# A selective scan on one core: the side chain of a unit moved to the first half of the unit ahead, and delta*u made by GpSimd

## The reference, cut to what matters

```python
xi, z = jnp.split(x @ in_w.T, 2, axis=-1)
xc = lax.conv_general_dilated(..., conv_w, (1,), [(D_CONV - 1, 0)], feature_group_count=D_INNER)
u = jnp.swapaxes(jax.nn.silu(xc + conv_b[None, :, None]), 1, 2)
x_dbl = u @ xproj_w.T                      # dt (8 columns), B (16), C (16)
delta = jax.nn.softplus(dt @ dt_w.T + dt_b)
A = -jnp.exp(Alog)
dA = jnp.exp(jnp.einsum('bld,dn->bldn', delta, A))
dBu = jnp.einsum('bld,bln,bld->bldn', delta, Bm, u)
h = a * h + b;  y_t = einsum('bdn,bn->bd', h, c)      # the scan, over t
y = y + u * Dp
return y * jax.nn.silu(z) @ out_w.T
# the block: out = concatenate([fw(x) + x, flip(bw(flip(x)) + flip(x))]) @ proj_w.T + proj_b, then a layer norm
```

## Time and profile before

| | us |
|---|---|
| median of 3 runs | 4233.08 |
| the profiled execution | 4230.57 |
| its span, first to last instruction | 4228.6 |
| VectorE busy in the span | 2663.5 (63%) |
| TensorE busy | 3369.4 (80%) |
| ScalarE busy | 1794.7 (42%) |
| GpSimd busy | 1184.5 (28%) |

### The profile page before, as it was taken

One profiled execution on the slowest core, in us unless ns is written; L12 is line 12 of the kernel. 1 busy time (PEld: TensorE's weight loads), 2 busy tenths in 40 slices (PEclk: granted clock), 3 DMA queues, 4 the chain that ended last, 5 costly groups with the idle time before them and its releaser, 6 DMA issues. The chain is left out here.

```text
span 4228.6 us, 48168 instructions
## 1 busy us (share of the span) xinstructions
PE 3369.4 (80%) x12573; PEld 1552.5 (37%) x12573; DVE 2663.5 (63%) x4056; ACT 1794.7 (42%) x2759; POOL 1184.5 (28%) x974
## 2 busy tenths in 40 slices
PE   5599986999985699877896777867777669558998
PEld 2122225444443354444443332323223243533443
DVE  6788854333345577554334999999999853454444
ACT  2166642444435255433333655556565413212222
POOL 3211110000002222100002888878888700100000
PEclk7699996999988799878897889888898969769999
DMA  4512110000006533100002333333333210000000
GB/s 136 124 59 65 54 41 1 0 0 0 0 28 172 128 93 87 47 0 0 0 0 82 127 124 121 134 116 130 120 131 122 98 38 0 2 0 0 0 0 20
DMA packets 131080, 253.84 MB, mean 60 GB/s; under 512 B 24773, under 2 KB 100954, under 8 KB 113434
## 3 DMA queue, kind: packets, MB, share of 16 engines
q1 hardware_dynamic: 126842, 250.55, 18.3%
q0 software_dynamic: 4096, 1.59, 0.2%
HBM read 191.98 MB, written 56.89 MB: 59 GB/s over the span
## 5 line engine op out<-in xcount | busy, mean ns | idle before, releaser
L1626 PE MATMUL a_y<-a_g,ident 128*128 128x512 f32 x1024 | 563.4, 687 | 275.9 <-POOL a_g L1906 256.9
L1906 POOL TENSOR_TENSOR a_g<-a_g,a_spread 128x1024 f32<-128x1024 f32 x256 | 662.2, 2600 | 176.1 <-DVE a_g L1839 174.3
L941 DVE TENSOR_REDUCE a_top<-a_sc 128x1 f32<-128x512 f32 (+3 forms) x1024 | 545.1, 585 | 168.9 <-PE a_sc L818 96.2
L1839 DVE TENSOR_TENSOR_SCAN a_g<-a_decay,a_drive 128x512 f32<-128x512 f32 x512 | 592.3, 1201 | 36.3 <-ACT a_drive L1756 35.5
L899 ACT ACTIVATE a_prob<-a_st 128x1024 f32<-128x1024 f32 (+2 forms) x512 | 419.1, 862 | 323.5 <-PE a_st L835 205.9
L455 DVE TENSOR_TENSOR f_s<-f_a,f_spread 128x512 f32<-128x512 f32 x392 | 268.0, 688 | 434.1 <-ACT f_a L440 268.7
L1626 PEld LDWEIGHTS a_y<-a_g,ident 128*128 128x128 f32 x1024 | 206.8, 213 | 605.6 <-POOL a_g L1906 364.5
L422 PE MATMUL f_y<-f_s,f_w 128*128 128x512 f32 x784 | 401.3, 599 | 21.2 <-DVE f_s L455 20.6
L415 PE MATMUL f_hid<-h,f_w 128*128 x784 | 403.8, 600 | 6.0 <-PEq L246 6.0
L1746 ACT ACTIVATE a_decay<-a_delta,a_capped_a 128x512 f32<-128x512 f32 x512 | 337.3, 713 | 123.7 <-DVE a_g L1839 65.5
L815 PE MATMUL a_sc<-a_k,a_q 96*128 96x512 bf16 (+3 forms) x1024 | 308.7, 357 | 41.2 <-DMA a_k<-a_k_rows 39.1
(11 more groups left out here) (329 smaller groups left out, 4930.6 us busy)
## 6 DMA issues: line engine op xcount, KB each, us to landing
a_spread<-a_bc_rows SPq DMA_DIRECT2D x128, 1024.0 KB, 4.6
a_q<-a_q_rows SPq DMA_DIRECT2D x64, 288.0 KB
a_pv_rows<-a_pv_sb SPq DMA_DIRECT2D x64, 256.0 KB, 2.1
a_q_rows<-p_qp SPq DMA_DIRECT2D x72, 128.0 KB
a_q_rows<-a1q_qp SPq DMA_DIRECT2D x72, 128.0 KB
a_k_rows<-a1q_kp SPq DMA_DIRECT2D x72, 128.0 KB
a_k<-a_k_rows SPq DMA_DIRECT2D x32, 288.0 KB
a_k_rows<-p_kp SPq DMA_DIRECT2D x72, 64.0 KB
```

The costliest lines, as they stand in the source:

```text
L941: nc.vector.tensor_reduce(top[:, t, n:n + 1], sc[:, slot(4 * n + t) % 3, 0:w], AX.X, ALU.max).then_inc(s.maxed, 1)
L1626: last = nc.tensor.matmul(y[:, k, :], S.ident[:, :], g[:, n % 8, k, :], start=(n == 0), stop=False)
L1839: nc.vector.tensor_tensor_scan(g[:, n % 8, k, way], decay[:, n % 4, k, way], drive[:, k, way], 0.0, ALU.mult, ALU.add).then_inc(scanned, 1)
L1906: nc.gpsimd.tensor_tensor(g[:, n % 8, :, :], g[:, n % 8, :, :], spread[:, pair % 4, 2 + n % 2:3 + n % 2, :].to_broadcast([P, H2, L]), ALU. ...
```

## The change

Nothing of the computation is changed, but where its steps stand.

- `dve_du` is gone. GpSimd's `du_s` (made at state 13 in place of 15) is copied by ScalarE to `du` in PSUM at the end of state 15 (`act_du`, new). The states drive from `du` as before.
- The side chain moves forward: conv of half 1 is made in the last four states of the unit before the one ahead, conv of half 0 in states 0 to 3; z, xproj, dpre on TensorE from states 7, 8, 9 to 4, 5, 6; ScalarE's silu, copy and soft from 7, 8, 9 to 6, 7, 8; squares and factors from states 10 to 13 to states 9 to 12; delta from after state 14 to after state 12.
- The output of the unit before moves back: out from state 4 to 9, o from 4 to 10, project from 5 to 11, the write to `h` from 6 to 14.

```diff
             def pe_unit(b, d, first, last_unit, ahead=True):
...
                 for n in range(STATES):
                     if n < TAPS and not last_unit:
                         if n == 0:
-                            nc.tensor.wait_ge(soft_read, 2 * U + 2)
-                        pe_conv(nb, nd, 1, (TAPS - 1 - n,))
+                            nc.tensor.wait_ge(soft_read, 2 * U + 1)
+                            wait(nc.tensor, o_done, U - 1)
+                            wait(nc.tensor, p_done, b - 1 if d == 0 else b)
+                        pe_conv(nb, nd, 0, (TAPS - 1 - n,))
...
+                    if not last_unit:
+                        if n == 4:
+                            pe_z(nb, nd, U + 1)
+                        if n == 5:
+                            pe_xproj(nd, U + 1)
+                        if n == 6:
+                            pe_dpre(nd, U + 1)
+                    if n == 9 and not first:
+                        nc.tensor.wait_ge(soft_read, 2 * U + (1 if last_unit else 3))
                         pe_out(U - 1, 1 - d)
-                    if n == 5 and not first and d == 0:
+                    if n == 11 and not first and d == 0:
                         pe_project(b - 1, U - 1)
...
+                    if ahead and n >= STATES - TAPS:
+                        if n == STATES - TAPS:
+                            nc.tensor.wait_ge(soft_read, 2 * U + 4)
+                        pe_conv(b + 1, d, 1, (STATES - 1 - n,))
...
             def act_silu(d, V):
+                wait(nc.scalar, y_done, V - 1)
...
+            def act_du(V):
+
+                nc.scalar.wait_ge(du_pooled, V + 1)
+                wait(nc.scalar, drive_done, H2 * (STATES * V - 1))
+                nc.scalar.activation(du[:, :, :], du_s[:, :, :], ACT.Copy).then_inc(du_done, 1)
...
-                    if n == 6 and not first and d == 0:
+                    if n == 14 and not first and d == 0:
                         nc.scalar.wait_ge(p_summed, b)
...
+                    if n == 6:
+                        act_silu(nd, U + 1)
                     if n == 7:
-                        act_silu(nd, U + 1)
+                        act_copy_xproj(U + 1)
                     if n == 8:
-                        act_copy_xproj(U + 1)
-                    if n == 9:
                         act_soft(nd, U + 1)
-                    if 10 <= n < 10 + len(LOG1P):
-                        act_square(U + 1, n - 10)
+                    if 9 <= n < 9 + len(LOG1P):
+                        act_square(U + 1, n - 9)
+                    if n == STATES - 1:
+                        act_du(U + 1)
...
-            def dve_du(d, V):
-
-                nc.vector.wait_ge(delta_done, V + 1)
-                wait(nc.vector, drive_done, H2 * STATES * V)
-                nc.vector.tensor_tensor(du[:, :, :], delta[:, d, :, :], u[:, d, :, :], ALU.mult).then_inc(du_done, 1)
...
-                    if n == STATES - 1 and not last_unit:
-                        dve_scan(U, d, n, lambda: dve_du(nd, U + 1))
-                    else:
-                        dve_scan(U, d, n)
+                    dve_scan(U, d, n)
...
-                    if n == 4 and not first:
+                    if n == 10 and not first:
                         dve_o(b if d == 1 else b - 1, nd, U - 1)
...
-                    if 10 <= n < 10 + len(LOG1P):
-                        dve_factor(nd, U + 1, n - 10)
-                    if n == 10 + len(LOG1P):
+                    if 9 <= n < 9 + len(LOG1P):
+                        dve_factor(nd, U + 1, n - 9)
+                    if n == 8 + len(LOG1P):
                         dve_delta(nd, U + 1)
...
             def pool_du(V, d):
...
+                wait(nc.gpsimd, du_done, V)
...
-                    if n == STATES - 1 and not last_unit:
+                    if n == STATES - 3 and not last_unit:
                         pool_du(U + 1, 1 - d)
```

More of the change, by code:

```diff
@@ L1677, in pe_dpre, with pe_unit @@
                                      start=True, stop=True).then_inc(dpre_done, 1)
-            def pe_unit(b, d, first, last_unit):
+            def pe_unit(b, d, first, last_unit, ahead=True):
                 U = 2 * b + d
@@ L1690, in pe_unit @@
                         pe_gate_sum(U - 1, 1 - d, STATES - LAG + n)
-                    if n == 4 and not first:
-                        nc.tensor.wait_ge(soft_read, 2 * U + 1)
+                    if not last_unit:
[7 more added lines that the diff above has]
+                        nc.tensor.wait_ge(soft_read, 2 * U + (1 if last_unit else 3))
                         pe_out(U - 1, 1 - d)
-                    if n == 5 and not first and d == 0:
+                    if n == 11 and not first and d == 0:
                         pe_project(b - 1, U - 1)
[L1696 to L1706, removed]
-                    if n == 9:
-                        pe_dpre(nd, U + 1)
+                    if ahead and n >= STATES - TAPS:
+                        if n == STATES - TAPS:
+                            nc.tensor.wait_ge(soft_read, 2 * U + 4)
+                        pe_conv(b + 1, d, 1, (STATES - 1 - n,))
             def act_silu(d, V):
+                wait(nc.scalar, y_done, V - 1)
                 for n, k in enumerate((1, 0)):
@@ L1830, in dve_drive, with dve_scan @@
                                             ).then_inc(drive_done, 1)
-            def dve_scan(U, d, n, between=lambda: None):
+            def dve_scan(U, d, n):
                 s = STATES * U + n
@@ L1840, in dve_scan @@
                                                  drive[:, k, way], 0.0, ALU.mult, ALU.add).then_inc(scanned, 1)
-                    if k == 0:
-                        between()
             def dve_gated(U, d):
@@ L1939, in _ @@
                 pe_dpre(0, 0)
+                pe.wait_ge(soft_read, 2)
+                pe_conv(0, 1, 1)
                 pe_unit(0, 0, True, False)
@@ L1944, in _ @@
                     pe_unit(i + 1, 1, False, False)
-                pe_unit(NB - 1, 0, False, False)
-                pe_unit(NB - 1, 1, False, True)
+                pe_unit(NB - 1, 0, False, False, False)
+                pe_unit(NB - 1, 1, False, True, False)
                 for n in range(STATES - LAG, STATES):
@@ L1958, in _ @@
                     act_square(0, q)
+                act_du(0)
                 act_unit(0, 0, True, False)
@@ L1973, in _ @@
                 dve_delta(0, 0)
-                dve_du(0, 0)
                 dve_unit(0, 0, True, False)
```

## The result

The changed kernel takes 4188.72 us (median of 4 runs, 4181.23 to 4196.43) against 4232.3 before (4 runs): a ratio of 0.9895, 95% interval 0.9875 to 0.9915. That is 44 us faster. Forecast were 90, with a range whose upper end was 4190. So the direction holds, and half of the gain is missing. The profiled execution is the slowest of the four, 4196.43 us.

What follows compares the result with a forecast made beforehand. VectorE was taken as the bound, idling 4.6 us a unit for square and drive. Fifteen units falling from 67.74 to 61.6 us give 92, less 2.3 at the start, 90 us: 4143 us, range 4120 to 4190.

Steps and rivals of the forecast that it cites:

- delta\*u leaves VectorE: VectorE no longer makes the product of delta and u, GpSimd's product serving instead: gain 2.4 us a unit.
- The copy, hidden at the hand-over: ScalarE's copy of du to PSUM, 1.14 us, hides behind scan 15: cost 0 a unit, 2.3 us once at the start.
- The chain starts earlier and both idle terms go: ScalarE's side chain one state earlier ends VectorE's idle for square and drive: gain 4.6 us a unit.
- the first rival: The chain is still late, VectorE keeping 2 us of idle a unit: 4173 us, chance 0.14.
- Turns with GpSimd: VectorE's factors and delta take turns with GpSimd's operations: 2.5 us a unit, ends 1.4 and 5.4.
- Work that VectorE keeps, 59.1 us, and the unit of 61.6: VectorE's remaining work is 59.1 us a unit; with 2.5 for turns the unit lasts 61.6, ends 60.5 and 64.5.

Runs made afterwards that it cites:

- experiment 3: The kernel before with only the product of delta and u taken from VectorE and copied by ScalarE at the unit's end: 4239.53 us, ratio 1.0028.
- Experiment 5: The changed kernel with VectorE's middle loop written out and two products by zero added on TensorE just before z: 4143.92 us, ratio 0.9795.
- experiment 1: The changed kernel with VectorE's loop over the middle six sequences written out, other engines keeping their loops: 4180.95 us, ratio 0.9897.
- experiment 4: The changed kernel with the product of delta and u given back to VectorE between the last scan's halves, no ScalarE copy: 4197.63 us, ratio 0.9929.

## Why the prediction was half right

*delta\*u leaves VectorE: right.* The row is gone. Its worth depends on the rest: alone it makes the kernel 11 us slower (experiment 3). With the chain moved it makes it 9 us faster by the medians (4197.63 to 4188.72), though the runs of the two touch (4195 to 4204, 4181 to 4196), and 5 by the stages (975.6 to 970.2), with five more slow z pairs in the second. Of the missing part 3 us at each branch is this step's: the product had covered it.

*The copy, hidden at the hand-over: right.* It took 1.01 us (1.14 taken). VectorE waits for it once, 3.5 us at the start; less the product's own 1.23 us that is the 2.3 us forecast. With delta left at state 14 it would have come 1.6 us late in each unit (experiment 3), so the copy needs the earlier chain.

*The chain starts earlier and both idle terms go: the failed step.* I laid square 0 at 32.0 to 33.3 us against a factor at 33.0, and wrote "idle 0 to 0.3", "I leave none". In a unit with a quick z pair that is so: in unit 7, which starts at 2767.42, the table load comes at 15.6 us as laid, the first square ends at 2799.34, at 31.9 us, and the factor starts at 32.9. The load costs 1.28 us and nothing besides (2783.02, with the Silu at 2784.32). But the estimate took the z pair at the speed of the old unit, where TensorE ran z without a gap in front of it. The move itself makes the gap, since TensorE now waits for u, and I counted that only as a gain ("some 1.3 would go"). Where TensorE's clock then falls at z, the pair and the sums behind it take 1.6 to 3.1 us more (1.8 in unit 5), and the room was 1 us. This term, which I put at nothing, is 29 us. I had this as the first rival, TensorE's lower clock included, at 0.14 and with 2 us a unit; it came in eight units, at 3.6.

*Turns with GpSimd: mis-sized.* I took 2.5 us a unit between 1.4 and 5.4. A clean unit has (1.42 + 1.69 + 1.19 + 2.25 + 3.25) - 5 x 1.19 = 3.85 less the 0.78 that the small operation gained, 3.1; a slow one has 1.5 to 3.0 more (the first, 0.7). What I missed is that a turn is a cliff: 0.74 us late at the factor turned into 1.5 more in it and 1.3 in the next. Wait and turns together are 3.5 to 3.6 us in each slow unit but the first, whether the square is 0.56 or 2.08 us late. GpSimd then works at 2.48 to 2.54 us an operation in the mean of a unit, far from the 3.08 at which it would bound the unit.

*Work that VectorE keeps, 59.1 us, and the unit of 61.6: right* for the unit that I described. Experiment 5, which takes away the two losses and nothing else, has units of 62.1 and takes 4143.9 us; the forecast was 4143. That the two agree to 1 us is in part luck: fourteen units are 0.5 us longer than I laid them, and the first, with no output to do, is 56.7 us, 4.9 shorter.

*The branch: missing altogether.* I looked at each wait on a semaphore and at no branch. After VectorE's last scan of a unit is released by drive 15 (its second half is copied from 2700.10 to 2700.70 in the trace after), the first drive behind the branch comes 4.5 us later. Before, the delta and the product lay between and covered it; now there are two halves of a scan, of which 1.6 us were left, and 2.9 show; 15 us in five units. That the writing-out removes it is shown (experiment 1). That it is the fetching of instructions is likely, from `issue` as the releaser and from the packet of instructions in each of the five idle times, but no run varies the fetching by itself.

## What to carry to other kernels

Moving a chain forward so that its consumer waits less makes its producer's engine wait more; on TensorE that wait can be paid again as a lower clock in the very products one is waiting for, as in eight of fifteen units here. A few products by zero in the wait, or a chain that starts one state sooner, cost less than that. Where two engines take turns, look at how far before the other's next start one asks: 0.7 us late can cost 3. And before work is taken out of the end of a loop's body, ask whether it covered the branch back.

## What the runs showed of the hardware

- TensorE, after 3.56 us without work, ran the z pair in 1.98 to 3.78 us (experiment 1 has both). The same wait gave either, and 1.86 us also gave either, so the gap in front doesn't tell it alone; the granted clock does, 0.50 to 0.78 over the slow pairs and 1.00 over the quick ones. What decides where in a unit the clock falls isn't shown. Over the whole stage it was 0.87 before and 0.90 after, so a mean doesn't show the loss. The four times of the changed kernel spread from 4181 to 4196 us, those of experiment 5 from 4142 to 4146.
- An operation of VectorE with two SBUF sources (1.19 us free) took up to 3.25 us beside GpSimd's products of 2.33. The GPSIMD Engine Reference of the Trainium skill (Key points) names such instructions as those that contend with GpSimd. The trace agrees: VectorE's drives, which have one source in PSUM, stayed at 683 ns in the mean in both kernels.
- The branch back of VectorE's loop cost 2.8 to 3.1 us where 1.6 us of work were left when the last scan was released, 0.3 to 0.6 where some 4 us were (experiment 4), and nothing in the kernel before, where 8 us were.
